# A state-space and feed-forward layer: the three looks at the weights of a block, and the loads that feed them, move to other places

## The reference

```
x = x + mixer(layernorm(x))     # 2 x 1024 x 512
x = x + ffn(layernorm(x))
mixer: proj = h @ W_in * mup -> z, xBC, dt;  xBC = silu(causal conv, 4 taps)
       dt = softplus(dt + dt_bias);  state = state * exp(-dt * exp(A_log)) + (dt * x) B
       y = state C + D x;  g = y * silu(z);  out = rmsnorm(g) * norm_w @ W_out
ffn:   (silu(h @ gate_w.T * gate_s) * (h @ up_w.T * up_s)) @ down_w.T * down_s
```

## Time and profile before

| | before |
|---|---|
| median of 3 runs | 778.66 us (771.44 to 779.11) |
| profiled execution | 775.15 us |
| its span, first to last instruction | 773.3 us |
| PE busy | 738.9 us (96%) |
| DVE / ACT / POOL busy | 522.8 / 492.1 / 293.0 us |
| mean granted PE clock | 0.989 of full |

### The profile page before, as it was taken

One profiled execution on the slowest core, in us unless ns is written; L12 is line 12 of the kernel. 1 busy time (PEld: TensorE's weight loads), 2 busy tenths in 40 slices (PEclk: granted clock), 3 DMA queues, 4 the chain that ended last, 5 costly groups with the idle time before them and its releaser, 6 DMA issues.

```text
span 773.3 us, 20312 instructions
## 1 busy us (share of the span) xinstructions
PE 738.9 (96%) x8486; PEld 609.9 (79%) x8486; DVE 522.8 (68%) x845; ACT 492.1 (64%) x933; POOL 293.0 (38%) x235
## 2 busy tenths in 40 slices
PE   4977999999999999999999998889999999999998
PEld 4855788888887887887888887678888888888887
DVE  6968976986987897797797697873633532642331
ACT  5989878977978977978879888634312321321330
POOL 2073275366457446627707618540010011001002
PEclk9988999999999999999999999999999999999999
DMA  9823144485475277366385369835113003002002
GB/s 300 233 66 110 30 114 118 86 246 133 83 206 175 80 159 215 87 149 195 76 219 184 83 187 320 232 102 159 42 56 109 0 28 136 0 14 91 5 1 84
DMA packets 42299, 94.97 MB, mean 123 GB/s; under 512 B 9888, under 2 KB 15776, under 8 KB 42016
## 3 DMA queue, kind: packets, MB, share of 16 engines
q1 hardware_dynamic: 42208, 93.67, 42.6%
HBM read 84.73 MB, written 17.57 MB: 132 GB/s over the span
## 4 chain that ended last, share of the span: by engine, by line
PE 52%; DVE 22%; ACT 17%; issue 7%; POOL 2%; DMA 1%; SPq 0%; DVEq 0%; ACTq 0%; POOLq 0%
PE ps_y L1691 10%; PE ps_proj L1678 10%; DVE cx L938 7%; PE ps_out L1678 6%; PE ps_x L1678 6%; ACT ring L717 3%; PE ps_proj L1224 3%; DVE ring L993 3%; PE ps_proj L1225 3%; PE ps_proj L1226 3%; ACT ring L721 2%; PE ps_x L1277 2%; PE ps_y L1300 2%; DVE dt_p L913 2%; POOL ring L532 2%
## 5 line engine op out<-in xcount | busy, mean ns | idle before, releaser
L532 POOL TENSOR_TENSOR ring<-tokd,ring 128x1024 f32<-128x1024 f32 x64 | 122.1, 1923 | 177.6 <-ACT tokd L712 124.4
L1224 PE MATMUL ps_proj<-xn_hi,win_x_hi 128*128 128x256 f32 x352 | 104.9, 298 | 2.6 <-DVE xn_lo L907 1.7
L1225 PE MATMUL ps_proj<-xn_lo,win_x_hi 128*128 128x256 f32 x352 | 100.3, 285 | 0.0
L1226 PE MATMUL ps_proj<-xn_hi,win_x_lo 128*128 128x256 f32 x352 | 99.9, 284 | 0.0
L938 DVE SCALAR_TENSOR_TENSOR cx<-cin,consts,cx 128x256 f32<-128x256 f32 x240 | 96.3, 476 | 0.0
L1547 POOL TENSOR_TENSOR res<-res,hidden 128x512 f32<-128x512 f32 (+1 forms) x16 | 20.1, 1257 | 166.3 <-DVE hidden L1610 165.3
L993 DVE TENSOR_TENSOR ring<-ring,ps_tok 128x1024 f32<-128x1024 f32 x64 | 75.6, 1214 | 7.8 <-ACT ring L721 7.6
L1224 PEld LDWEIGHTS ps_proj<-xn_hi,win_x_hi 128*128 128x128 f32 x352 | 67.8, 193 | 15.8 <-issue 12.4
L717 ACT ACTIVATE ring<-ring 128x1024 f32<-128x1024 f32 x64 | 66.8, 1060 | 15.3 <-POOL ring L532 15.3
L1224 PE MATMUL ps_proj<-xn_hi,win_z_hi 128*128 128x256 f32 x256 | 73.9, 289 | 0.0
L1225 PE MATMUL ps_proj<-xn_lo,win_z_hi 128*128 128x256 f32 x256 | 72.3, 282 | 0.0
(11 more groups left out here) (186 smaller groups left out, 1889.9 us busy)
## 6 DMA issues: line engine op xcount, KB each, us to landing
ring<-cum_dram SPq DMA_DIRECT2D x128, 256.0 KB, 5.2
xin<-x SPq DMA_DIRECT2D x8, 512.0 KB, 3.7
res<-x SPq DMA_DIRECT2D x32, 128.0 KB, 2.8
x_dram<-res SPq DMA_DIRECT2D x32, 128.0 KB, 2.9
res<-x_dram SPq DMA_DIRECT2D x16, 256.0 KB, 2.7
out<-res SPq DMA_DIRECT2D x15, 256.0 KB, 2.1
x_in_sb<-x_dram SPq DMA_DIRECT2D x3, 1024.0 KB, 5.6
gate_w_copy<-gate_w SPq DMA_DIRECT2D x4, 704.0 KB, 6.6
```

The costliest lines, as they stand in the source:

```text
L532: pool.tensor_tensor(ring[:, g, :, :], own, ring[:, g, :, :], ALU.subtract).then_inc(diffed, 1)
L1224: pe.matmul(out, hi[:, k, :], xn_hi[:, k, :], start=(k == 0), stop=False)
L1225: pe.matmul(out, hi[:, k, :], xn_lo[:, k, :], start=False, stop=False)
L1226: made = pe.matmul(out, lo[:, k, :], xn_hi[:, k, :], start=False, stop=(k == KT - 1))
```

## The change

The wait for the looks and the place of the loads and of the looks change; what is computed stays the same. On DVE the looks at the parts of block i leave block i + 1 (two at its head, one behind its first gate) and stand together behind block i's own first gate, in the order 2, 1, 0. On SP the parts 2 and 1 are issued behind the tables of groups 0 and 1 of step 1, part 0 between those of groups 2 and 3. Part 1 now waits for the first step's carry (`STEPS * i`). The wait at the head of `body(i)` is for all three looks of the block before.

```
             def load_low_rows(i):
-                sp.wait_ge(carry_added, STEPS * i + 1)
+                sp.wait_ge(carry_added, STEPS * i)
...
                 if i - 1 in LOOKED:
-                    sp.wait_ge(hand.low_max_made, 3 * (i - 2) + 1)
+                    sp.wait_ge(hand.low_max_made, 3 * (i - 1))
...
-                for g in range(GROUPS):
-                    load_cums(i, 1, g)
+                load_cums(i, 1, 0)
+                load_cums(i, 1, 1)
+                if i in LOOKED:
+                    load_low_buf(i)
+                    load_low_rows(i)
+                load_cums(i, 1, 2)
+                if i in LOOKED:
+                    load_low_xin(i)
+                load_cums(i, 1, 3)
...
-                if i in LOOKED:
-                    load_low_xin(i)
-                    load_low_buf(i)
-                    if i >= BLOCKS - 3:
-                        keep_weights(COPIES - (BLOCKS - 1 - i))
-                else:
+                if i >= BLOCKS - 3:
+                    keep_weights(COPIES - (BLOCKS - 1 - i))
+                if i not in LOOKED:
                     load_x(i + 2)
...
                 load_whole(i + 1, False)
-                if i in LOOKED:
-                    load_low_rows(i)
...
                 if not first:
                     gate_lo(c - 1)
-                if i - 1 in LOOKED:
-                    low_max(i - 1, 0)
-                    low_max(i - 1, 1)
                 make_xpad(i, 0)
...
                 gate(i, 0)
-                if i - 1 in LOOKED:
-                    low_max(i - 1, 2)
+                if i in LOOKED:
+                    for n in (2, 1, 0):
+                        low_max(i, n)
```

## The result

| | before | after |
|---|---|---|
| median (runs side by side, 6 of each) | 775.08 us (771.44 to 779.11) | 785.16 us (781.80 to 792.81) |
| ratio to before | | 1.0147, 95% interval 1.0105 to 1.0189 |
| profiled execution, its span | 775.15, 773.3 us | 785.63, 783.9 us |
| PE / DVE / ACT / POOL busy | 738.9 / 522.8 / 492.1 / 293.0 us | 742.6 / 530.1 / 491.6 / 295.0 us |
| mean granted PE clock | 0.989 | 0.982 |

The change made the kernel 1.5% slower, about 10 us; the forecast was 774.9 us in a range of 768 to 781. It was wrong in its sign. (The forecast stood on a median of 778.66 us from three runs; over six it is 775.08. As a change it said 3.8 us less, and 10.1 us more were measured.) The spans of the two profiled executions differ by 10.6 us. Measured from one head's `gate_lo` to the next, the blocks 1 to 6 last 378.2 us in place of 364.2, 14.0 us more.

What follows compares the result with a forecast made beforehand. Each block's chain was read as ACT, then PE, then DVE (12, 19, 29 of 60 us). Three blocks by 1.0 us plus 0.8 in block 7 gave 3.8 us less than 778.66: 774.9 us, range 768 to 781.

Steps and rivals of the forecast that it cites:

- The head: Two looks leave each block's head, 2.3 us of DVE in ACT's part; DVE's wait for ACT grows instead: worth nothing.
- That rival: Looks at the six heads were on the path, 2.3 us each, 13.8 us in all: 764.9 us; chance 0.08.
- SP's wait and the first table: Without SP's wait, step 1's first table is issued 1.6 us earlier; blocks 2, 4 and 6 gain 1.0 us each.
- The table comes too early: Rival, blocks 2 to 6: POOL's early differences hold DVE's two normalising instructions of x; 789.4 us, chance 0.05.
- The parts among the tables: 1.4 MB between 239 and 249 us need 4.0 us of DMA, delaying the fourth table 0.8 us, to about 251.5.
- `xin` lands at 249 to 251: Block 3: the part in `xin`, issued at 244.4 us, should land then; its look wants it at 251.3.
- a part or the fourth table comes too late: Rival: late fourth table or `xin` part costs 1.7 us in six blocks, 10.2 less 0.8: 788.1 us; chance 0.07.
- It decides from a delay of 2 us: The delay of a part or the fourth table from which that slower rival was said to decide.
- both margins: Block 3: fourth table expected about 251.5, allowed 253.1; `xin` at 249 to 251, wanted 251.3; each under 2 us.
- Block 7: It loses all three looks; the third stood before `make_xpad`, for which PE waited 0.79 us: 0.8 us gained.

Runs made afterwards that it cites:

- e4: Kernel before, with the two copies at a block's head issued ahead of SP's wait on the look; 770.52 us, ratio 0.9965.
- e3: Changed kernel with the parts in `xin` and `rows` cut to 128 columns, 64 KB instead of 512 KB; 769.81 us, ratio 0.9945.
- e2: Changed kernel with the part into `xin` issued behind the fourth table instead of ahead of it; 780.22 us, ratio 1.0094.
- e1: Changed kernel whose third look reads `rows` a second time, so DVE doesn't wait for the part in `xin`; 783.17 us, ratio 1.0127.
- e8: e4 with the 512 KB part for `xin` issued between the tables of groups 2 and 3, its look left at the next head; 772.94 us.
- e5: Changed kernel with the three dt steps on DVE moved behind `make_xpad` and `mask_cb`; 790.48 us, ratio 1.0220.
- e6: e1 with the three dt steps also moved behind `make_xpad` and `mask_cb`; 792.61 us, ratio 1.0294.
- e9: Changed kernel with POOL's fourth difference of the second step held until DVE's three dt steps are done; 785.44 us, ratio 1.0155.
- e10: Changed kernel with the edits of e1 and e2 together; 779.85 us, ratio 1.0106.

## Why the prediction was wrong, point by point

**The head.** "Worth nothing" for the two looks was right: from the head to the end of the fourth `mix` are 12.95 us before and 12.94 to 13.16 after. That rival is out.

**SP's wait and the first table.** Right in the main. The stores of step 0 landed in 2.3 to 2.4 us in five of the six blocks (before in up to 6.1), the first difference of the blocks 2 to 6 starts 16.9 to 18.0 us behind the head (before 17.9 to 20.0; in block 6 nothing is gained), and e4 fits the 3 us that the forecast gave for it: 3.7 us in the medians, with six equal blocks.

**The table comes too early.** It didn't: the two L901 instructions (L903 after the change) still take 1.00 us at 244.28 in block 3 of after, and start 15.6 to 15.9 us behind the head in all six blocks. The lock that this rival feared was there all the same, but at the dt steps.

**The parts among the tables.** This is the step that failed: "Between none of the 4.0 us and all of it ahead of that table I take 0.8, since most falls in gaps". The fourth table was forecast to land 26 us behind the head. Before, it landed at 25.1 to 26.1 us in the six blocks; after, at 27.8 to 32.4, which is 4.1 us later in the mean (2.1 in block 1, 7.1 in block 6): all of it, and not 0.8. In block 3 it is 5.2 us (25.1 and 30.3). Some 1.8 of these are a later issue, since PE freed the buffer that much later, and 3.5 lie between issue and landing (3.95 and 7.41 us). Two numbers were wrong in that sentence, and one thing was left out:

- The gaps. The windows of before show 1.84 us of free DMA engines from 238 to 246, and 3.6 us up to 250. The forecast took the share of 0.90 of the earlier trace rows, where the parts pass alone, and no share of the stretch into which they were to go.
- The rate. I took 348 GB/s from a stretch in which only parts passed, which is 387 GB/s per full share. Tables with two residual loads (237 to 245 us) move 187 GB/s at a share of 0.65, 290 per full share. Mixed, 243 to 257 us, it was 243 GB/s at 0.94: 260 per full share. Summed over windows of 2 us, the 16 engines were busy for 8.4 us with the tables before (238 to 252) and for 14.8 with tables and parts after (240 to 260), so the parts cost some 6 us and not 4.0.
- The order. Gaps of 3.6 us could have held most of 4.0 us, but all three parts are issued ahead of the last table (at 249.15 us at the latest, the last table from 250.86 on). So what of them does not fit a gap passes ahead of it.

**`xin` lands at 249 to 251.** Wrong by the same sum: issued 20.7 us behind the head, `xin` landed 8.64 us later, 29.4 behind it (block 3), where 23.5 to 25.5 had been forecast. DVE waited 11.8 us for it in six blocks.

**The rival that happened** is the last one, given 0.07: "a part or the fourth table comes too late", with 788.1 us; 785.2 were measured. Its mechanism, transfers too large for their place, is confirmed by e3. Of its two halves e2 bears out the late table; for the late part there are 11.8 us of waits in the trace, but e1's gain is not clear of noise. It had "1.7 us in six blocks"; the blocks 1 to 6 grew by 14.0 us, 2.3 each, and 2.9 came back from block 7 on, where 0.8 were forecast. That the time came near its 788.1 is in part luck, since both terms were too small. "It decides from a delay of 2 us" fits: e8's delays of up to 2.1 us cost little, the 4 us of after cost 2.3 a block. The fault was its chance, not its working: both margins were known to be under 2 us, and the delay to set against them was chosen, not bounded.

**What it missed.** A late fourth table does not only wait for itself. It shifts all of POOL's following work, and the small dt steps on DVE are held wherever they meet it: 0.93 us becomes 1.4 to 3.8 us in the changed kernel. The wait for `xpad` that follows had a second price that no rival counted, PE's half clock. The Trainium skill (SBUF — State Buffer, "Who interferes with whom") says that a DVE instruction with two SBUF inputs contends with a GpSimd one that reads SBUF. The traces agree: the dt steps, which read `dt_p` and `dt_e`, are held (4.89 against 2.57 us), while `g_lo`, with one input in PSUM, takes its usual 1.21 us beside a difference at 447.78.

**Block 7.** Its gate ends 3.9 us earlier behind its head, and 2.9 us of this last to the end of the span, instead of 0.8. The look is gone from the front of `make_xpad`, and its two normalising instructions, which took 4.30 us before, took 2.59:

```profile
500.18 2.59 DVE L1160 TENSOR_SCALAR xin<-xin,moments,rstd 128x512 f32<-128x512 f32 x2 [1.17 <-POOL rstd L574]
```

In e1, e2 and e3 they are held as before (4.17 us), and block 7 ends its gate at 40.8 to 42.9 us instead of 38.3. So part of this gain hangs on how POOL happens to stand, and is not the change's own.

**What stays open.** Why tables and parts together run at a lower rate than either, by the share of the engines, was not tried. Nor do the runs give one price each for the late part and the late table: taken away, they give 2.0 and 4.9 us alone, 5.3 together of the 15.3 that the volume costs. The rest is in the late third table, POOL's hold and PE's clock, and these were not priced one by one.

## What to carry to other kernels

Before a load is put among others on a full queue, read the share of the DMA engines in exactly that stretch, count what is free before the next deadline and what stands ahead of that deadline's load in the queue, and take the rate of that stretch and not that of a quiet one. If the margin is under 2 us and the volume needs 4, it is not a small risk but the forecast. A wait taken away may uncover another engine's lateness behind it: here only less data, or data at another time, helped, and each of the three reorderings of the victims (e5, e6, e9) left the hold or moved it.

## What the runs showed of the hardware

A short pause can cost PE twice. Block 2 of after, windows as above: PE waits 1.76 us for `xpad`, and is granted 0.50 behind it (1.2 GHz in place of 2.4), so the carry, the eight products behind `xpad`, takes 3.19 us, 1.94 otherwise:

```profile
198.00:200.00 2.00, 0.64 (x4) 0.36 (x6) 2.00 (x5) 2.00 (x5) 1.80 (x3) 0.98 0.00 0
200.00:202.00 2.00, 2.00 (x7) 0.25 (x3) 1.22 (x2) 2.00 (x3) 1.31 (x1) 0.50 0.31 73
```

```profile
199.36 3.19 PE L1277 MATMUL ps_x<-state,cx 128*64 128x512 f32 x8 [1.76 <-DVE xpad L981]
```

The same befell blocks 5 and 6 of this trace (waits of 1.81 and 3.17 us; the carry takes 2.79 and 3.46 us). The length of the pause alone does not decide it: the clock stayed full behind 2.53 us in e1 and 2.11 us in e10, and fell behind 0.79 us in block 7 of before (carry 3.06 us).

A DMA's landing was its place in the queue more than its size: 64 KB behind the tables landed after 7.5 us, 512 KB in the same place after 9.6.
